# A two-layer relational graph attention kernel: W1 times the logit columns with the columns stationary, and a second attention with its attention weights stationary

## The reference, cut to what matters

```python
def rgat_conv(x, W, q, k, b, src, dst, etype, heads, out_ch, n_nodes):
    xr = jnp.einsum('nd,rdf->rnf', x, W)
    oi = xr[etype, dst]
    oj = xr[etype, src]
    alpha = jax.nn.leaky_relu(oi @ q + oj @ k, 0.2)
    m = jax.ops.segment_max(alpha, dst, num_segments=n_nodes)
    e = jnp.exp(alpha - m[dst])
    z = jax.ops.segment_sum(e, dst, num_segments=n_nodes)
    a = e / (z[dst] + 1e-16)
    msg = (a[:, :, None] * oj.reshape(-1, heads, out_ch)).reshape(-1, heads * out_ch)
    return jax.ops.segment_sum(msg, dst, num_segments=n_nodes) + b

h = jax.nn.elu(rgat_conv(x, W1, q1, k1, b1, ..., 4, 192, n))
out = rgat_conv(h, W2, q2, k2, b2, ..., 1, 768, n)
result = _layernorm(x + out)
```

## Time and profile before

| what | us |
|---|---|
| median of 3 runs | 1352.9 |
| the profiled execution, its own time | 1352.16 |
| its span, first to last instruction | 1350.4 |
| first one-hot tile of the pair loop (DVE) | 49.45 |
| first step of the second attention (PE) | 1011.25 |
| end of its last step | 1329.07 |

### The profile page before, as it was taken

How to read it: one execution, slowest core, us unless ns; L and a number is a source line. 1 busy time by engine, 2 the same in 40 slices (tenths; PEclk the granted TensorE clock), 3 DMA queues, 4 the chain that set the end, 5 groups by cost and what they waited for, 6 DMA issues and landing times.

```text
span 1350.4 us, 19310 instructions
## 1 busy us (share of the span) xinstructions
PE 1295.7 (96%) x7042; PEld 1168.5 (87%) x7042; DVE 1069.7 (79%) x1447; ACT 769.7 (57%) x1291; POOL 6.5 (0%) x21
## 2 busy tenths in 40 slices
PE   7989999999989999999999999999979999999995
PEld 6876665666669999999999999999969999999994
DVE  1579989999939989989989976868736667867874
ACT  3345542322159979979979964238534445555552
POOL 1000000000000000000000000000000000000000
PEclk9689999999999999999999999999999999999997
DMA  9212013111153333333333226964477866677561
GB/s 324 72 71 89 24 43 123 47 49 49 37 203 98 104 98 98 99 97 98 100 94 95 63 66 199 294 217 155 165 228 258 271 219 203 218 238 237 190 208 38
DMA packets 84984, 188.38 MB, mean 140 GB/s; under 512 B 8221, under 2 KB 59230, under 8 KB 84898
## 3 DMA queue, kind: packets, MB, share of 16 engines
q1 hardware_dynamic: 84608, 186.49, 41.8%
q0 software_dynamic: 192, 0.57, 0.1%
q10 hardware_dynamic: 98, 0.16, 0.0%
HBM read 147.59 MB, written 39.61 MB: 139 GB/s over the span
## 4 chain that ended last, share of the span: by engine, by line
PE 79%; DVE 13%; ACT 4%; DMA 2%; issue 2%; SPq 0%; ACTq 0%; DVEq 0%
PE ps L1129 23%; PE ps L1074 23%; PE ps L910 14%; PE ps L933 9%; PE ps L984 4%; DVE arena L1254 2%; PE ps L892 2%; DVE arena L1310 2%; PE ps L880 2%; DMA arena<-in_L_gnn_W 1%; DVE arena L1314 1%; ACT arena L686 1%; ACT arena L687 1%; DVE ps L1382 1%; DVE misc L1264 1%
## 5 line engine op out<-in xcount | busy, mean ns | idle before, releaser
L1074 PE MATMUL ps<-arena 128*128 128x193 f32 x2400 | 398.1, 328 | 1.8 <-DVE arena L1314 1.5
L1074 PEld LDWEIGHTS ps<-arena 128*128 128x128 f32 x2400 | 393.6, 190 | 4.2 <-DVE arena L1314 3.6
L910 PE MATMUL ps<-arena,xT 128*128 128x384 f32 (+1 forms) x720 | 246.2, 490 | 0.2 <-issue 0.2
L686 ACT ACTIVATE arena<-arena,misc 128x640 f32<-128x640 f32 x240 | 197.2, 822 | 30.9 <-DVE arena L1310 23.1
L910 PEld LDWEIGHTS ps<-arena,xT 128*128 128x128 f32 x720 | 131.6, 190 | 78.6 <-issue 2.3
L1310 DVE TENSOR_TENSOR arena<-arena 128x1280 f32<-128x1280 f32 x120 | 178.3, 1486 | 24.8 <-ACT arena L687 23.8
L687 ACT ACTIVATE arena<-arena,misc 128x640 f32<-128x640 f32 x240 | 196.1, 817 | 0.0
L1314 DVE SCALAR_TENSOR_TENSOR arena<-arena,Ct 128x1280 f32<-128x1280 f32 x120 | 179.2, 1493 | 14.0 <-DVE arena L1310 9.4
L1129 PE MATMUL ps<-g_hi,x2a 128*128 128x416 f32 (+1 forms) x540 | 155.4, 357 | 10.2 <-DVE g_lo L1469 8.8
L1254 DVE SCALAR_TENSOR_TENSOR arena<-arena,misc 128x1250 f32<-128x1250 bf16 x108 | 155.7, 1510 | 2.2 <-ACT arena L638 2.2
L1129 PE MATMUL ps<-g_hi,x2b 128*128 128x416 f32 (+1 forms) x540 | 152.2, 351 | 0.0
(11 more groups left out here) (172 smaller groups left out, 1479.4 us busy)
## 6 DMA issues: line engine op xcount, KB each, us to landing
x2a<-xr_d SPq DMA_DIRECT2D x41, 768.0 KB, 4.4
x2b<-xr_d SPq DMA_DIRECT2D x41, 768.0 KB, 4.4
arena<-xr_d SPq DMA_DIRECT2D x120, 193.0 KB, 2.4
xr_d<-stg SPq DMA_DIRECT2D x60, 384.0 KB, 3.2
arena<-ab_d SPq DMA_DIRECT2D x12, 1280.0 KB, 6.3
xr_d<-bb SPq DMA_DIRECT2D x60, 193.0 KB, 2.4
arena<-in_L_gnn_W SPq DMA_DIRECT2D x5, 2304.0 KB, 9.6
arena<-in_L_gnn_W SPq DMA_DIRECT2D x7, 1152.0 KB, 6.9
```

The costliest lines, as they stand in the source:

```text
L686: nc.scalar.activation(e1[t % 5][:, h, :], abr[:, r, h, :], ACT.Exp, bias=qk1t[:, t, col + R * H:col + R * H + 1])
L910: last = mm(unit1_bank(u)[:, 0:w], xT[:, kt, t * P:(t + 1) * P], v, start=kt == 0, stop=kt == KT - 1)
L1074: last = mm(bank1(g, i)[:, o:o + HD + 1], e1[t % 5][:, h, i * P:(i + 1) * P], xring[t % NX][:, o:o + HD + 1], start=False, stop=True, skip ...
```

## The change

**W1 times columns.** `wq_product` exchanges its operands: the 8 columns of `qv1` are stationary and the 128 columns of the transposed W1 tile stream, so the result is 8 rows by 128. Six k tiles of a relation collect in banks 6 and 7; ACT copies 8 x 768 once for a relation (`wqs`), PE turns it back with six small transposes (`wq_transposes`), and ACT writes 48 columns in one instruction (`wq_columns`). Eight tiles stand ahead of the pair loop instead of ten; the other ten are transposed at every pair 2.5 on average, the last at pair 22. The transposes of x take turns in three banks instead of two.

**Second attention.** The attention weights are stationary, 128 targets at a time, and the source block streams, 384 or 386 columns. The parts are groups of 4, 3 and 3 target tiles (the last of 98). Two columns of ones behind each source block give the denominators, so `zacc`, `oT`, the copies of six banks and the transposes back go. The result of a target tile lies in a pair of banks (`TILE_BANKS`) and DVE reads it there. `rows2` of all tiles of a part stands behind step 1 of the next part. All 90 source blocks are loaded, in ten buffers in turn, each 2 x 776 columns wide instead of 2 x 768. The ones are written to memory by two transfers ahead of the first attention's loads.

```diff
-    XW = 2 * F
-    CUTS = [(112, 112, 112, 80), (112, 112, 112, 80), (112, 112, 98, 96)]
+    XO = 8
+    XW = 2 * (F + XO)
+    CUTS = [(128, 128, 128, 128), (128, 128, 128), (128, 128, 98)]
...
-        KEPT = [5, 12, 19, 26]
-        NRING = NX2 - len(KEPT)
         def x2_slot(s):
-            ...
+            return s % NX2, s // NX2 + 1
...
-        OUT_AT = [2, 5, 8, 11]
-        ROWS_AT = [j + 4 for j in OUT_AT]
+        ROWS_AT, STAT_AT, BIAS_AT = 1, 3, 24
+        TILE_BANKS = ((0, 1), (2, 7), (4, 5), (6, 3))
+        TILE_PAIR = [(0, 1, 2, 3), (0, 1, 2), (3, 0, 1)]
...
-        PRE = 10
-        WT_AT = {3 * (i - PRE): i for i in range(PRE, R * KT)}
+        PRE = 8
+        WT_AT = {5 * (i - PRE) // 2: i for i in range(PRE, R * KT)}
...
             sp.dma_start(b1b[:, :], b1.rearrange("(a f) -> a f", a=1).broadcast_to([P, F])).then_inc(S["bias_in"], 16)
+            for a in range(2):
+                sp.dma_start(xr2_d[:, :, a, F:F + XO].rearrange("n p c -> p n c"), onesf[:, :].unsqueeze(1).broadcast_to([P, RS, XO])).then_inc(S["wide_out"], 16)
...
             def wq_out(i):
-                act.wait_ge(S["wq_done"], i + 1)
                 r, kt = i // KT, i % KT
-                o = wqk1[:, kt, :].rearrange("p (a r h) -> p a r h", a=2, r=R)[:, :, r, :]
-                nc.scalar.activation(o, ps[6 + i % 2][:, 0:2 * H].rearrange("p (a h) -> p a h", a=2), copy).then_inc(S["wq_ready"], 1)
+                if kt == KT - 1:
+                    act.wait_ge(S["wq_done"], i + 1)
+                    for b in range(2):
+                        last = nc.scalar.activation(wqs[0:2 * H, b * HF:(b + 1) * HF], ps[6 + b][0:2 * H, 0:HF], copy)
+                    last.then_inc(S["wqs_ready"], 1)
+                if kt == 1 and r:
+                    wq_columns(r - 1)
...
                 for ft in range(KT):
-                    last = mm(ps[6 + i % 2][:, 0:2 * H], WT[i % 2][:, ft * P:(ft + 1) * P], qv1[:, ft, :],
+                    last = mm(ps[6 + kt // 3][0:2 * H, kt % 3 * P:(kt % 3 + 1) * P], qv1[:, ft, :], WT[i % 2][:, ft * P:(ft + 1) * P],
                               start=ft == 0, stop=ft == KT - 1)
                 last.then_inc(S["wq_done"], 1)
+                if r and kt == 1:
+                    wq_transposes(r - 1)
+
+            def wq_transposes(r):
+                pe.wait_ge(S["wqs_ready"], r + 1)
+                for kt in range(KT):
+                    last = nc.tensor.transpose(ps[7][:, HF + kt * 2 * H:HF + (kt + 1) * 2 * H], wqs[0:2 * H, kt * P:(kt + 1) * P], ident[0:2 * H, 0:2 * H])
+                last.then_inc(S["wq_tr"], 1)
...
-                    for k in range(KT):
+                    for i, (d0, d1) in enumerate(SUBS[g]):
+                        c, k = d0 - PARTS[g][0], d1 - d0
+                        banks = tile_banks(g, i)
                         if g and j == 0:
-                            pe.wait_ge(S["ot_act"], KT * (g - 1) + k + 1)
-                        for m, (x_, a) in enumerate(((xs[:, k * P:(k + 1) * P], hi), (xs[:, k * P:(k + 1) * P], lo), (xs[:, F + k * P:F + (k + 1) * P], hi))):
-                            last = mm(ps[k][:, 0:w], x_, a, start=j == 0 and m == 0, stop=j == RS - 1 and m == 2)
+                            p = TILE_PAIR[g][i]
+                            q = max(q for q in range(g) if p in TILE_PAIR[q])
+                            pe.wait_ge(S["o_sum"], M0[q] + TILE_PAIR[q].index(p) + 1)
+                        hi, lo = (v[n % NG][:, c:c + k] for v in (g_hi, g_lo))
+                        for m, (a, x0) in enumerate(((hi, 0), (hi, F + XO), (lo, 0))):
+                            for b in range(2):
+                                wide = HF + 2 if b and x0 == 0 else HF
+                                last = mm(banks[b][0:k, 0:wide], a, xs[:, x0 + b * HF:x0 + b * HF + wide], start=j == 0 and m == 0, stop=j == RS - 1 and m == 2)
...
-                z = zacc[g % 2][:, 0:w]
-                ...
-                    V.tensor_tensor(z, z, v, ALU.add).then_inc(S["z_acc"], 1)
...
-                        if j + 1 in ROWS_AT:
-                            bias2(g - 1, ROWS_AT.index(j + 1))
-                        if j in ROWS_AT:
-                            rows2(g - 1, ROWS_AT.index(j))
-                            statistics(g - 1, ROWS_AT.index(j))
+                        if j == ROWS_AT:
+                            for i in range(NS[g - 1]):
+                                rows2(g - 1, i)
+                        if STAT_AT <= j < STAT_AT + NS[g - 1]:
+                            statistics(g - 1, j - STAT_AT)
```

More of the change, by code:

```diff
@@ L241, in rgat @@
         g1 = [take(PART) for _ in range(NG)]
-        g2 = [take(PART) for _ in range(2)]
         assert pos[0] <= AT_A1
         pos[0] = AT_RAW
-        zacc = [take(PART) for _ in range(2)]
-        assert pos[0] <= AT_RAW + NP
-        pos[0] = AT_RAW + NP
         g_hi = [take_r(f"g_hi{i}", PART) for i in range(NG)]
@@ L354, in rgat @@
         NB_X = 3 * KT
+        XBK = (0, 1, 3)
         def bank1(g, i):
@@ L553, in _ @@
                     load_ab2(g, R - 1)
-                if g and STORE_AT <= j < STORE_AT + NSUB:
+                if g and STORE_AT <= j < STORE_AT + NS[g - 1]:
                     store_out(sp, g - 1, j - STORE_AT)
-            for i in range(NSUB):
+            for i in range(NS[LAST]):
                 store_out(sp, LAST, i)
-            sp.wait_ge(S["o_out"], 16 * NSUB * NPART)
+            sp.wait_ge(S["o_out"], 16 * M0[NPART])
         @block.gpsimd
@@ L989, in _ @@
                     wq_product(WQ_AT[pair])
+                if pair == max(WQ_AT) + 1:
+                    wq_transposes(R - 1)
                 for n in steps0(pair):
```

193 lines of the change are left out of this document (85 added, 108 removed).

## The result

The changed kernel takes 1341.98 us in the median of 11 executions (1340.96 to 1346.11), the kernel before beside it 1348.78 (11, 1346.66 to 1354.49). The ratio is 0.9942, its 95% interval 0.9927 to 0.9956. In a later comparison (experiment 0) it was 0.9967 (0.9954 to 0.9980). So the kernel is faster by 0.33 to 0.58%, some 4.5 to 8 us, where 16 were forecast. The two profiled executions are further apart, 1341.47 and 1352.16 us, 10.7 us; experiment 11 shows why.

What follows compares the result with a forecast made beforehand. PE holds 79% of the chain and DVE 13%, so terms count where either is last. Terms -5.5 - 8.0 + 0.7 + 0.8 + 4.0 - 8.3 + 0 = -16.3 take 1352.2 to 1336 us; range 1326 to 1352.

Steps and rivals of the forecast that it cites:

- Start of the loop, -5.5: Start of the pair loop: earlier DVE unpacking (-1.1) and a shorter wait for PE's flag (-4.4), -5.5 us.
- The loop, -8.0: Pair loop to pair 26: turned product holds PE at 2.4 GHz, 48.5 us instead of 56.5, -8.0 us.
- The formula 26 x 1.0 + 10 x 0.66 + 12 x 1.28 = 48.0: Pair loop at full clock: 26 pairs at 1.0 us, plus tile transposes and products, 48.0 us before corrections.
- waits shared with the denser tiles take off about 2: Pair loop: a credit of about 2 us because the denser tiles share waits with the pairs.
- Behind pair 26, +0.7: After pair 26: one more of 60 steps of x W1 is left there, +0.7 us.
- The second attention, +4.0: Its 90 steps: matmuls +9.7, output groups gone -6.5, waits at part changes +1.2, DVE relief -0.4, +4.0 us.
- the 6.5 of the output groups: Second attention: eight output groups removed, 0.81 us each, -6.5 us.
- Tail, -8.3: After the last step: first division starts earlier (5.15 us saved), one tile fewer (3.2 us), -8.3 us.
- Start, +0.8: Start of the second attention: first part 512 wide instead of 416 lengthens PE's wait, +0.8 us.
- Loads: Rival, 8%: loads bound the second attention, costing 5 to 10 us if 6208-byte rows are much dearer, 1343 us.
- cheap repeated weights: Rival, 6%: second attention pays overhead only where the stationary tile changes, 18.6 us less, 1317 us.
- The ones, 0: Ones transfers ahead of first attention's loads: hidden at 16.6 ns a piece, 0 us; rival of a stall, 6%, 1372 us.

Runs made afterwards that it cites:

- experiment 0: The changed kernel again, unaltered, on another chip for a second profile: 1343.99 us, 0.9967 of the kernel before.
- experiment 11: The kernel before the change again, unaltered, for a second profile: 1346.31 us in the profiled execution.
- experiment 1: The changed kernel with its early stage undone (8 columns streamed, old tile places), second attention as changed: 1345.58 us, 0.9953 of the kernel before.
- experiment 2: The changed kernel's early stage with the second attention as in the kernel before: 1347.86 us, 0.9969 of the kernel before.
- experiment 3: The changed kernel with the old tile places, ten ahead of the pair loop and the rest at every third pair: 1340.81 us, 0.9916 of the kernel before.
- experiment 4: The changed kernel with the old product (8 columns streamed) at the new tile places: 1346.55 us, 0.9961 of the kernel before.
- experiment 9: experiment 7 with the last product at pair 23 and ScalarE's copy of the last columns at pair 25, ahead of the units: 1330.15 us, 0.9851.
- experiment 6: experiment 3 with the flag's sum and the release of the one-hot rows ahead of the tenth tile: 1338.04 us, 0.9922 of the kernel before.
- experiment 5: The changed kernel with each product three pairs behind its transposes instead of two, first unit one pair later: 1338.45 us, 0.9925 of the kernel before.
- experiment 7: experiment 6 with each pair-loop product cut into two halves in successive pairs, first unit at pair 26: 1335.27 us, 0.9884 of the kernel before.
- experiment 8: The changed kernel with eight transfers of ones instead of two, the extra six into unread buffers: 1355.78 us in one execution.
- experiment 10: experiment 7 repeated unaltered because one of its executions took 4186.79 us: 1334.26 us, 0.9878 of the kernel before.

## Why the forecast was right in direction and too far in size

**Start of the loop, -5.5, was -3.7.** The step that failed is the landing of the second fetch at 30.7. I took the start of its issue, 24.42, over from the profile before. After the change it starts at 25.64, because the first fetch, which it waits for, was slower: issued at 14.71 and used by VectorE at 20.84 before, issued at 14.35 and landed at 22.04 now.

```profile
14.71 0.91 POOL L580 DMA_INDIRECT arena<-code_d,smalli  x1 [0.31 <-issue]
20.84 0.73 DVE L1165 TENSOR_SCALAR_CACHE_REDUCE arena<-arena,small 80x500 f32<-80x500 f32 x1 [8.39 <-DMA arena<-code_d,smalli]
```
```profile
25.64 0.90 POOL L582 DMA_INDIRECT arena<-code_d,smalli  x1 [0.30 <-issue]
```

The 6.3 us from the start of the issue to landing were right (6.39, landed at 32.03). The first fetch took 6.7 to 7.7 us in the other profiles, 7.4 in the kernel before itself in experiment 11, so the 6.1 of the profile I read was a fast one. VectorE was 1.9 us later than I had it: 1.2 from the issue, 0.1 from the flight, and most of the rest from the transposes of the edge rows, 1.06 us at half clock instead of 0.6. The wait for the flag shrank as said, from 4.83 to 0.37 us.

**The loop, -8.0, was -3.3.** That the clock would go up was right, and experiments 1 to 4 show its cause. Its worth hangs on the draw of the kernel before: against the 51.8 us of experiment 11 the same loop is 1.4 us longer, so that the forecast came as near as it did is partly luck. The formula 26 x 1.0 + 10 x 0.66 + 12 x 1.28 = 48.0 was too: the twenty full pairs with eight tiles come to 35.5 by it, and measure 36.28 with one set of small transposes and more in them. What failed is the "waits shared with the denser tiles take off about 2": there is no such credit. The first three pairs take 10.53 us instead of 8.2 (half clock after the 2.32 us pause), and the last three 6.38 instead of 4.3 (ScalarE's 1.44). Together 4.7 us: 2.0 of credit, 0.9 more for the cold start than the 1.5 I allowed, and 1.9 in the middle and at the end beyond the 1.0 for small transposes. A pause of PE can cost twice in this stage, in itself and in the clock after it (experiment 9); the 0.87 us of each period cost only themselves.

**Behind pair 26, +0.7, was +1.8**: the 0.87 us wait ahead of the first unit, for the copy of the turned columns, was not in the sum. ScalarE's copy ends at 102.02 and the unit starts at 102.11; before, PE waited 0.22 us there.

**What I did not weigh** is the places. I priced two tiles more in the loop at 3.8 us and two fewer ahead of the flag at up to 4.4, as nearly even. Experiment 3 has them 0.8 to 1.7 us in favour of the old places; experiment 6 shows that the flag can be early with both.

**The second attention, +4.0, was +3.5**: 1800 x 0.1752 = 315.4, so +8.7 rather than +9.7; the changes of part waited 1.16 + 0.67 = 1.8 us rather than 2.6 (+0.4 over before), and with the 6.5 of the output groups taken as forecast, 0.9 us are left over that no run divides. The first step at half clock is not their source: its 24 matmuls are 2.6 us over the later pace, and the 18 of the kernel before (1011.25 to 1017.50) were 2.8 over theirs. **Tail, -8.3, was -8.9. Start, +0.8, was 0.** **Loads** of 776 KB landed in 4.3 to 4.5 us and nobody waited: that rival is out, and so is the one of cheap repeated weights, by the same 0.1752. **The ones, 0, were 0.** The 7922 packets of 392.5 to 400 us took 88.4% of 16 engines, 13 ns each (14 to 15 with four times as many), near the 16.6 I took from short reads. The Trainium skill ("DMA: Bandwidth & Descriptors", Specifications) warns of pieces under 512 bytes because they are read, modified and written; here 32 bytes cost no more than other short pieces do, and no longer piece is in the comparison.

**The clock and transposes.** The Trainium skill ("TensorE: Matmul & The Clock Gate", Part 4) has transposes not count as activity. This case's traces do not agree. In the changed kernel PE waits 7.72 us up to 32.08 and then does nothing but transposes until 39.6 (lines 969, 976 and 878); the granted clock is 0.50 until 35 us and 1.00 from 36. In run 0 it goes up at 37 to 38 us in the same way. So transposes alone can bring the full clock, as I read the stretch from 27.00; the turned product need not be what raises the clock, and what the runs show of it is that beside it the clock falls only behind a pause of PE.

## What to carry to other kernels

Where a stage runs between two clock levels, a profile of one execution is one draw: take the spread of the medians, or a second profile, before a term is priced from it. In such a stage allow for a pause of the matrix engine costing twice, and look at where another engine's copy stands in its order before moving work. Work that must be done beside a loop paced by another engine is best cut to pieces that fit into each turn; a piece twice as long, in every third turn, is partly lost.

## What the runs showed of the hardware

- Beside the same f32 product the clock held at 2.4 GHz when the small operand (8 columns) was stationary and 128 columns streamed (1.48 us for 12 records), and often fell to 1.2 GHz when the 8 columns streamed (2.57 us in this view, but 1.40 in experiment 1). Ten profiles of the one and four of the other agree: granted clock in the loop 0.94 to 1.00 against 0.70 to 0.80.
- In the kernel before the clock fell at 44.6 us without any pause of PE, from a transpose set of 0.85 us to one of 1.52.
- Pauses of 1.44 and 0.87 us at the loop's end, 1.3 us of work between them, were followed by half clock for 6 to 7 us in five profiles (experiments 2, 5, 7, 8 and 10) and not in four (the changed kernel, 0, 3 and 6); the one pause of 0.82 us in 9 was not.
- Transposes alone were followed by the rise of the clock: 0.50 until 35 us, 1.00 from 36, in the changed kernel.
- An indirect fetch landed 6.0 to 7.7 us after the start of its issue (profiles of the kernels before and after).
- After the 8.86 us wait the first 24 matmuls of the second attention take 6.76 us (1005.95 to 1012.71) instead of 4.2.
- Writes of 32 bytes to memory cost 13 to 15 ns each on one of 16 engines.
